# Moving group steps to later tiles in a graph network kernel of two relational layers and three mean layers

## What is computed

```python
# two relational layers
for l in range(2):
    W = einsum('rb,bio->rio', coeff[l], basis[l])       # 8 matrices of 256 x 256
    all_h = einsum('ni,rio->rno', h, W)
    h = segment_sum(all_h[etype, src] * norm, dst) + bias[l]   # relu after the first
x = layernorm(x + h)
# three mean layers between an input and an output product
h = x @ W_in + b_in
for l in range(3):
    agg = segment_sum(h[src], dst) / degree
    h = relu(agg @ W_agg[l] + h @ W_self[l] + b_hid[l])
out = layernorm(x + h @ W_out + b_out)
```

## Time and profile before

| | us |
|---|---|
| runs | 1959.12, 1962.34, 1962.52; median 1962.34 |
| profiled execution | 1962.86, of it the span from first to last instruction 1961.0 |
| PE busy | 1707.9 (87% of the span) |
| DVE busy | 1229.3 (63%) |
| POOL busy | 1275.7 (65%) |
| ACT busy | 495.2 (25%) |

### The profile page before, as it was taken

One profiled execution on the slowest core, in us unless ns is written; L12 is line 12 of the kernel. 1 busy time (PEld: TensorE's weight loads), 2 busy tenths in 40 slices (PEclk: granted clock), 3 DMA queues, 4 the chain that ended last, 5 costly groups with the idle time before them and its releaser, 6 DMA issues.

```text
span 1961.0 us, 32300 instructions
## 1 busy us (share of the span) xinstructions
PE 1707.9 (87%) x10003; PEld 1424.5 (73%) x10003; DVE 1229.3 (63%) x4083; ACT 495.2 (25%) x1040; POOL 1275.7 (65%) x1307
## 2 busy tenths in 40 slices
PE   5687788988889988888889989999988889999997
PEld 4666676777777776676777777777777777777775
DVE  8978767786777777576777755454554554322344
ACT  2012121211121112122232225444112212533332
POOL 7777777777777777777777777777777775000011
PEclk9989999999999999999999989999998999999999
DMA  8334454444344334444444446554444442210011
GB/s 265 105 111 120 131 151 110 116 109 112 109 114 109 110 110 116 116 133 127 126 138 120 132 129 166 159 147 137 123 117 123 124 131 79 77 50 0 11 41 46
DMA packets 148682, 223.13 MB, mean 114 GB/s; under 512 B 79261, under 2 KB 104508, under 8 KB 148508
## 3 DMA queue, kind: packets, MB, share of 16 engines
q0 software_dynamic: 61152, 166.68, 30.3%
q1 hardware_dynamic: 51260, 40.65, 7.0%
q10 hardware_dynamic: 36096, 13.70, 2.6%
HBM read 203.66 MB, written 17.27 MB: 113 GB/s over the span
## 4 chain that ended last, share of the span: by engine, by line
PE 58%; DMA 24%; POOL 9%; issue 4%; DVE 4%; DVEq 0%; ACT 0%; ACTq 0%; POOLq 0%
PE bank L1163 21%; DMA RY<-H,si 12%; DMA RY<-in_x,si 12%; PE bank L1005 10%; PE bank L1426 9%; POOL RY L390 9%; PE bank L725 3%; PE bank L1055 2%; PE bank L988 2%; PE bank L1392 2%; PE bank L1436 2%; PE bank L1498 1%; PE bank L987 1%; DVE RY L669 1%; PE bank L1070 1%
## 5 line engine op out<-in xcount | busy, mean ns | idle before, releaser
L1163 PE MATMUL bank<-RY 128*128 128x128 f32 x5088 | 737.8, 288 | 191.2 <-DMA RY<-in_x,si 106.0
L1163 PEld LDWEIGHTS bank<-RY 128*128 128x128 f32 x5088 | 665.4, 198 | 272.6 <-DMA RY<-in_x,si 127.7
L390 POOL DMA_INDIRECT RY<-in_x,si x627 | 639.0, 1019 | 194.5 <-issue 142.6
L390 POOL DMA_INDIRECT RY<-H,si x630 | 599.3, 951 | 191.9 <-issue 142.0
L669 DVE TENSOR_SCALAR RY<-iot,c,wgt 128x128 f32<-128x128 f32 x1290 | 451.6, 360 | 320.7 <-PE bank L1163 319.2
L834 ACT CAST RY<-bank 128x320 uint8<-128x320 f32 x215 | 91.1, 424 | 559.1 <-PE bank L988 539.5
L1426 PE MATMUL bank<-Ar,hs 125*128 125x500 f32 x800 | 203.9, 405 | 0.0
L661 DVE TENSOR_TENSOR RY<-RY,bank 128x256 f32 x430 | 179.4, 417 | 38.5 <-issue 26.0
L547 DVE TENSOR_SCALAR RY<-iotN,bcol 128x320 bf16<-128x320 f16 x645 | 201.9, 313 | 0.0
L1487 POOL TENSOR_TENSOR x1b<-x1b,bo 125x256 f32<-125x256 f32 x20 | 14.7, 735 | 273.2 <-DMA x1b<-X 273.2
L1005 PE MATMUL bank<-RX,RY 128*128 128x256 f32 x704 | 182.5, 387 | 7.5 <-issue 3.7
(11 more groups left out here) (159 smaller groups left out, 1536.7 us busy)
## 6 DMA issues: line engine op xcount, KB each, us to landing
RY<-H,si POOLq DMA_INDIRECT x630, 2.8
RY<-in_x,si POOLq DMA_INDIRECT x627, 2.8
Ad<-RY ACTq DMA_DIRECT2D x215, 40.0 KB
A<-Ad SPq DMA_DIRECT2D x22, 312.5 KB, 3.4
D<-Ad SPq DMA_DIRECT2D x14, 305.2 KB
RX<-in_basis ACTq DMA_DIRECT2D x2, 2048.0 KB, 20.0
AhG<-Ad SPq DMA_DIRECT2D x6, 610.4 KB
H<-RY SPq DMA_DIRECT2D x23, 128.0 KB
```

The costliest lines, as they stand in the source:

```text
L390: e.indirect_dma_start(G[0:k, slot, :], None, table, bass.IndirectOffsetOnAxis(ap=index[0:k, t:t + 1], axis=0)).then_inc(s_land[slot], 16)
L1163: mm = e.matmul(bank[2 + wg % 3][:, c * 128:(c + 1) * 128], rows, S[0:k, n % NSS, :], start=(i == 0 and not ahead), stop=(i == TA - 1))
```

## The change

Two plans give other tile numbers. In layer one all ten steps of windows 1 to 19 stand two tiles later. In layer two, for windows 0 to 15, step 10 stands one tile later, step 11 four, step 12 five and step 13 eight. The units of groups 0 to 7 begin eight tiles later, those of group 7 being five tiles apart instead of six, and with the units move the casts of their blocks. All other numbers, the instructions themselves and their data are the same.

```diff
+LATE = {10: 1, 11: 4, 12: 5, 13: 8}
...
             first, by = (41, 1) if l == 0 and g == 0 else (end + 4, 2) if g < NW - 2 else (end + 3, 1)
+            late = LATE if l == 1 and g < 16 else {}
+            if l == 0 and 0 < g < NW - 2:
+                first += 2
             for k in range(10 if l == 0 else 14 if g < NW - 2 else 11):
-                tile = end + 2 + (k + 1) // 2 if l == 0 and g == NW - 2 else first + by * k
+                tile = end + 2 + (k + 1) // 2 if l == 0 and g == NW - 2 else first + by * k + late.get(k, 0)
...
     for gi in range(LASTG):
-        first, by = (92 + 60 * gi, 6) if gi < 8 else (572, 3) if gi == 8 else (602, 2)
+        first, by = (100 + 60 * gi, 6 if gi < 7 else 5) if gi < 8 else (572, 3) if gi == 8 else (602, 2)
```

## The result

Over 20 runs of each kernel the changed one takes 1964.73 us (median, 1961.89 to 1968.38), the kernel before 1962.04 us: a ratio of 1.0016, with a 95% interval of 1.0010 to 1.0022. It is 2.7 us slower by the medians and 2 to 4 us by the interval. That is inside the forecast range and under the 0.2% that the forecast took as the limit of what can be told from no change, but it is clear of the noise and not the "no effect" that the forecast put first. The profiled execution of the changed kernel took 1968.38 us, the slowest of the 20; the kernel before's took 1962.86. So the profile shows more (5.6 us of span) than the medians do (2.7).

What follows compares the result with a forecast made beforehand. The prediction took POOL's unbroken row of gathers to bound the first 84% of the span, with an untouched tail behind. Its terms summed 0 + 0 + 0 + 0, so 1962.3 us, range 1957 to 1968.

Steps and rivals of the forecast that it cites:

- no effect: Whole run: the change leaves the time at 1962.3 us, with a phase spread of 1.5 us; chance 0.66.
- What bounds the kernel: First 84% of the span: one unbroken row of gathers on POOL; PE could give back only 1.1 us.
- PE is the bound: Rival: 12.7 us of PE waits lie on the path, so the run takes 1949.6 us; chance 0.05.
- POOL gets blocked: Rival: PE falls behind, POOL's gathers wait for slots, 1970 to 1974 us; chance 0.07.
- Layer two, units and blocks: Layer two's moved steps, units and casts: value 0; PE's 9.6 us of transpose waits mostly go, gathers stay late.
- The held load of A: Layer two: SP stops for a slot freed at tile 144 + 60m, formerly 136; value 0.
- The boundary: Between the layers: POOL's 1.7 us stall for window 20's H1 store stays; value 0, ends -1.7 and +1.7.
- The end of layer two: Last 60 us before the tail, which hang on PE: value 0, ends -1.1 and +3.7; shift's chance 0.10.
- POOL against DVE: DVE instructions with two SBUF inputs lengthen gathers: value 0, 1.5 us phase spread, ends 11 us either way.
- the tail: Sign: from the last sum to the end, untouched by the change, should take 312 to 313 us.
- The last gather: Sign, end of layer two: starts at 1644 give or take 3 us; over 4 us away means wrong.
- POOL's beat meets DVE otherwise: Rival: shifted DVE phase costs -6 or +6 us, 1956 or 1968; chance 0.12 for 4 us or more.

Runs made afterwards that it cites:

- e3: Kernel before with the hot tiles' compared sources moved to PSUM, so L711 has one input in SBUF: 1931.66 us, ratio 0.9823.
- e2: Kernel before with only layer two's steps, units and blocks moved, layer one unchanged: 1966.50 us, ratio 1.0001.
- h1d: Kernel before with layer one's steps two tiles later and the bias add reading its first input from PSUM: 1962.53 us, ratio 1.0002.
- e1: Kernel before with only layer one's steps two tiles later, layer two unchanged: 1970.12 us, ratio 1.0020.
- g1b: Kernel before with layer one's steps three tiles later, layer two unchanged: 1962.58 us, ratio 1.0004.
- e4: Changed kernel with the hot tiles' compared sources moved to PSUM: 1933.12 us, ratio 0.9828.
- f1: Kernel before with layer one's steps two tiles later and hot sources in PSUM: ratios 0.9928 and 0.9920, on devices where the kernel before took 2257 and 2281 us.
- h1: Kernel before with layer one's steps two tiles later and the bias add reading PSUM, where the kernel before took 2257 us: ratio 0.9996.

## Why the prediction was wrong

*What bounds the kernel: right.* POOL has no stall in either trace, and each microsecond of gather is a microsecond of the run: e3 gives back 34.8 us of gather time in layer one against e2 on the same device (640.4 - 605.6) and 34.9 us of time. The rival that PE is the bound fell, the one that POOL gets blocked too.

*Layer two, units and blocks: 0, right.* e2 has ratio 1.0001 (0.9991 to 1.0012). The transposes' waits went (9.6 to 0.3 us) and turned into waits for rows. The held load of A had no consequence that a wait shows.

*The boundary: 0, right.* 1.7 us before and after.

*The end of layer two: inside the bounds, cause open.* The last sum starts 3.9 us behind the last gather before, 5.1 after, 3.0 in e2, 5.6 in h1d, whose layer two is that of the kernel before. All of this is inside the bounds of -1.1 and +3.7. But the four profiles with layer one's steps two tiles later have 4.2 to 6.1 us there, and the four others 3.0 to 3.9. Up to 1 or 2 us of the loss may thus arise at that end and not in the gathers; no run tests it, and one profile of each kernel doesn't tell it from chance. Since e2, with layer two's edit, shows no loss, it would be a consequence of layer one's two tiles all the same.

*POOL against DVE: this step failed.* The prediction knew the mechanism and took 0, "as the phases of the trace are as good as random", and of the bias adds it said that "they already fall on gathers now". They did not, in the sense that counts: each overlapped a gather in time, but only 1 of 21 lengthened one by over 0.2 us. I had bounded them by number times length (8 us), given them the value 0, and not looked at where in POOL's 1.25 us beat each begins. Counted from the start of the last gather, the 21 adds begin mostly at 0.0 to 0.2 and 0.6 to 0.7 us before; with two tiles more they crowd at 0.8 us, where they cost nothing, and at 1.2 us, just ahead of the next gather, where they cost 0.2 to 0.3 us each (one add before, four after, seven in e1). So the phase of the adds is no draw: in four profiles with the old place or three tiles, 1, 1, 2 and 2 gathers are lengthened by over 0.2 us, and in three with two tiles, 6, 8 and 6. My reading of the program is that DVE's queue waits for sums of three tiles, the sums wait for landings, and landings follow POOL's own issue, so that the beat repeats every three tiles; a step moved by two tiles changes its place in it, by three it keeps it. g1b fits this and no run contradicts it, but no run was made to show the chain of waits itself. The term was 0 and measured 1.3 to 1.7 us in the profiles (0.49 to 1.93 and 2.23; 0.65 to 1.91 in e3 and e4). The prediction's "the one thing that lengthens a gather is a DVE instruction with both inputs in SBUF" was also too narrow, as L547 shows, though this cost it nothing here.

*How much is left.* By time, the bias add's edit takes layer one's loss from 1.0020 to 1.0002, 3.5 us with an uncertainty of nearly 3, the two runs being on different devices, each against the kernel before there; by profile it took away 2.1 us (2.23 in e1 to 0.12). So the adds may be the whole of the change's 2.7 us or about half of it. The 18 long L711 are no proven rest: the gathers beside them cost 36.0 and 37.0 us in two profiles with layer one as before, 37.5, 36.6 and 37.2 us in three with two tiles more, 34.7 in g1b. These scatter within the spread of 1.5 us that the prediction gave them, and with L692 added the two groups overlap. Where the rest lies, if there is one, is open: f1 against e3 on one undisturbed device would have told for L711, and was not had.

*The number and the signs.* The time lies inside the range because the range left room for the phase of L711, which is not shown to be what moved it; that the time is inside is luck. Of the signs that were named, POOL's waits, PE's waits for the normalised rows (0.3 us) and the tail (312.6 us) came as forecast. The last gather at 1648.81 us is 4.35 us away from 1644.46, beyond the 4 us that were named as a sign of being wrong, in the slowest of the 20 runs. The rival "POOL's beat meets DVE otherwise" named the right engine pair, but its 6 us came from L711 alone.

*The rule that was weighed.* The page "SBUF — State Buffer" of the Trainium skill, section "Who interferes with whom", infers that a tensor_tensor with two SBUF inputs spares descriptor generation. e3 and h1d contradict it with one operand moved to PSUM: the gather beside the instruction falls from up to 3.57 us to 0.95, and from 1.20 us to 0.95. Its rule that the shared ports are an exclusive lock agrees with the trace (the gather ends 0.8 us behind the DVE instruction). Whether it is the gather's writing of descriptors or its reading of indices that is held up, no run shows.

## What to carry to other kernels

Where POOL's indirect DMAs are one unbroken row, as here, a DVE instruction with two inputs in SBUF can be on the path, by the part of it that runs while a gather wants to begin; give one of the inputs a place in PSUM, and look for the longest such instruction first. Moving steps about won nothing in this kernel and lost through the phase: count, for the moved DVE instructions, how many begin just ahead of a gather, before calling them hidden. A difference of 0.15% took 20 runs of each to show here; one profile each would have told the wrong size (5.6 us for 2.7).

## What the runs showed that was not expected

One operand's place was worth 1.8% of a tuned kernel: 1966.5 to 1931.7 us, at an unchanged 2.83 us for the DVE instruction. A short DVE instruction (0.41 us) costs a gather 0.2 to 0.3 us if it begins just ahead of it, and in four cases (two after, one each in e1 and e4) 0.38 to 0.43 us where it began 0.08 to 0.14 us behind its start. Other adds at 0.08 to 0.1 us cost only 0.04 to 0.06 us; what makes the difference is not shown.

The kernel before took 1962 to 1967 us on some devices and 2257 to 2282 us on others, with a mean granted TensorE clock of 0.90 instead of 0.97. In the chain of waits of h1's profile there, 13% of the span lies outside the core's shown work:

```profile
PE 63%; another core or an unknown queue 13%; DVE 10%; issue 8%; ACT 3%; DVEq 1%; ACTq 1%; DMA 0%; POOL 0%; POOLq 0%
```

No experiment was made on its cause.
